# Sending the expert share with the routed row, and summing a token's four rows on TensorE

## The reference

```python
probs = softmax(x @ router_w + router_b)          # 16 experts
topw, topi = top_k(probs, 4)
topw = topw / sum(topw)
for each expert e:                                 # all of them on all tokens, in the reference
    acc += (gelu(x @ w1[e] + b1[e]) @ w2[e] + b2[e]) * combine[:, e]
x = layernorm(x + acc)
```

## Time and profile before

| | |
|---|---|
| median of 3 runs | 784.97 us (783.91 to 785.06) |
| the profiled execution | the page gives its span alone, 781.0 us from the first to the last instruction |
| PE / PEld busy | 583.7 us (75%) / 468.7 us (60%) |
| DVE busy | 576.7 us (74%) |
| ACT / POOL busy | 404.8 us (52%) / 348.8 us (45%) |
| DMA | 54.64 MB, 70 GB/s on the mean |

### The profile page before, as it was taken

How to read it: one execution, slowest core, us unless ns; L and a number is a source line. 1 busy time by engine, 2 the same in 40 slices (tenths; PEclk the granted TensorE clock), 3 DMA queues, 4 the chain that set the end, 5 groups by cost and what they waited for, 6 DMA issues and landing times.

```text
span 781.0 us, 18314 instructions
## 1 busy us (share of the span) xinstructions
PE 583.7 (75%) x4172; PEld 468.7 (60%) x4172; DVE 576.7 (74%) x1999; ACT 404.8 (52%) x1107; POOL 348.8 (45%) x445
## 2 busy tenths in 40 slices
PE   4576888778657899999999988239999999993000
PEld 1355666666546677777777756128888888883000
DVE  4888898898535788888988975676666666652998
ACT  1456654556224666666666653027666666663111
POOL 2611111011001137667667775637777777775000
PEclk9687787667656999999999985559999999998555
DMA  5000001000073012122121111243333333333653
GB/s 176 0 15 14 15 13 31 4 0 0 1 215 88 15 35 62 57 60 60 55 60 53 41 49 51 73 99 81 96 97 101 98 101 97 93 100 82 219 193 99
DMA packets 62705, 54.64 MB, mean 70 GB/s; under 512 B 16748, under 2 KB 52146, under 8 KB 62416
## 3 DMA queue, kind: packets, MB, share of 16 engines
q1 hardware_dynamic: 52816, 36.86, 17.1%
q0 software_dynamic: 8704, 16.87, 6.9%
q10 hardware_dynamic: 1152, 0.53, 0.3%
HBM read 29.96 MB, written 21.11 MB: 65 GB/s over the span
## 4 chain that ended last, share of the span: by engine, by line
PE 48%; DVE 19%; DMA 11%; issue 11%; SPq 4%; ACT 3%; POOL 2%; DVEq 1%; POOLq 0%; ACTq 0%
PE bank L781 6%; DMA ys<-yout,xin 5%; PE bank L788 4%; DMA xin<-xs 4%; PE bank L655 4%; PE bank L664 4%; PE bank L629 3%; PE bank L620 3%; DVE r L1450 3%; PE bank L646 3%; PE bank L539 3%; PE bank L773 2%; DVE Rq L1101 2%; DVE mx L1251 2%; PE bank L556 2%
## 5 line engine op out<-in xcount | busy, mean ns | idle before, releaser
L498 POOL DMA_INDIRECT ys<-yout,xin x144 | 145.8, 1013 | 54.4 <-issue 38.2
L479 POOL DMA_INDIRECT xs<-xrow,slots x128 | 130.5, 1019 | 50.7 <-issue 43.5
L996 ACT ACTIVATE hid<-bank,wcur 128x128 f32<-128x128 f32 x292 | 91.4, 364 | 41.1 <-PE bank L781 40.3
L781 PE MATMUL bank<-xinT,wcur 128*128 128x128 f32 x584 | 100.3, 295 | 0.6 <-issue 0.2
L1406 DVE COPY wcur<-wall 128x642 f32 x148 | 74.9, 508 | 20.9 <-DVE gates L1397 0.9
L788 PE MATMUL bank<-wcur,hid 128*128 128x128 f32 x576 | 88.5, 277 | 0.0
L1251 DVE TENSOR_REDUCE mx<-bank 128x4 f16<-128x308 f32 x128 | 60.0, 469 | 33.5 <-PE bank L629 31.9
L781 PEld LDWEIGHTS bank<-xinT,wcur 128*128 128x128 f32 x584 | 77.8, 194 | 8.5 <-issue 3.2
L1413 DVE TENSOR_TENSOR yout<-bank,wcur 128x128 f32<-128x128 f32 x144 | 42.0, 291 | 53.3 <-PE bank L788 51.9
L931 ACT ACTIVATE Ex<-bank 77x512 f32<-77x512 f32 x128 | 75.2, 588 | 5.1 <-PE bank L646 4.4
L788 PEld LDWEIGHTS bank<-wcur,hid 128*128 128x128 f32 x576 | 76.7, 194 | 0.0
(11 more groups left out here) (212 smaller groups left out, 1355.2 us busy)
## 6 DMA issues: line engine op xcount, KB each, us to landing
xin<-xs SPq DMA_DIRECT2D x156, 64.5 KB, 1.8
yin<-ys SPq DMA_DIRECT2D x16, 512.0 KB, 3.7
ys<-yout,xin POOLq DMA_INDIRECT x144, 2.3
xTg<-xT_dram SPq DMA_DIRECT2D x8, 256.0 KB, 2.8
X<-x_dram SPq DMA_DIRECT2D x1, 2048.0 KB, 8.3
x1s<-X SPq DMA_DIRECT2D x32, 64.0 KB
wall<-w_dram SPq DMA_DIRECT2D x1, 2048.0 KB, 8.5
X<-xrow SPq DMA_DIRECT2D x32, 64.0 KB
```

Of the source, the lines that this page charges most:

```text
L479: pool.indirect_dma_start(words, bass.IndirectOffsetOnAxis(ap=slots[p][:, r:r + 1], axis=0), xrow[p][:, r, 0:RW], None).then_inc(s(f"scatt ...
L498: pool.indirect_dma_start(ys, bass.IndirectOffsetOnAxis(ap=xin[p][:, :].bitcast(U32)[:, E:RW], axis=0), yout[p][:, :], None, bounds_check= ...
L781: mm = pe.matmul(psH[p % 3][:, c * P:(c + 1) * P], wcur[p % QUAD][:, c * P:(c + 1) * P], xinT[p % 4][:, :], start=True, stop=True)
L996: act.activation(hid[p % 3][:, c, :], psH[p % 3][:, c * P:(c + 1) * P], ACT.Gelu, bias=wcur[p % QUAD][:, 2 * I + c:2 * I + c + 1]).then_in ...
```

## The change

The share is carried with the row. `RW` becomes E + 2 = 130: column E keeps the row number and column E + 1 holds exp(logit - greatest logit), not yet divided by the sum. VectorE's copy into `topl` becomes a subtraction of the greatest logit, and ScalarE writes the exponential into `xrow` in a new piece `shares`, once per block; GpSimd's scatter waits for that too. In stage 3 VectorE computes b2 times the share for a tile (`b2u`, new) and then evicts psum times share plus `b2u` in one scalar_tensor_tensor. The rows in `ys` are thereby weighted.

In stage 4 TensorE sums the four weighted rows of a token: four matmuls with the identity as weights, 256 columns (two blocks) each, accumulated in one PSUM bank of four. VectorE multiplies the sum by the reciprocal sum of shares and adds `X`, takes the statistics and computes -mean x deviation (`nm3`); ScalarE normalises with Identity, scale and bias. `yin` gets six buffers in place of four, `r3`, `mv3`, `rs3` four, and all engines' programs of this stage are written out 16 times rather than looped. SP's order is: load f + 6, store f. Two of the VectorE instructions ahead of stage 3 and a wait between VectorE and ScalarE go.

```diff
-        RW = E + 1
+        RW = E + 2
...
             for f in range(YB):
                 load_y(f)
             for f in range(NF):
                 if f + YB < NF:
                     load_y(f + YB)
                 store(f)
...
                 pool.wait_ge(s("slots_ready"), b + 1)
+                pool.wait_ge(s("share_ready"), b + 1)
...
+            def expert_sum(f):
+                pe.wait_ge(s(f"y_in{f % YB}"), 16 * (f // YB) + 16)
+                free(pe, "gathered", FB * (f - 3))
+                for j in range(TOP):
+                    mm = pe.matmul(banks[f % 4][:, 0:FB * E].rearrange("p (c e) -> p c e", c=FB), ident[:, :], yin[f % YB][:, :, j * E:(j + 1) * E],
+                                   start=(j == 0), stop=(j == TOP - 1))
+                mm.then_inc(s("sum_ps"), 1)
...
+            def shares(i, c):
+                b, p = 4 * i + c, c % 4
+                act.wait_ge(s("top_saved"), b + 1)
+                act.activation(xrow[p][:, :, E + 1:E + 2], topl[:, bass.ds(b, 1), :].rearrange("p b k -> p k b"), ACT.Exp).then_inc(s("share_ready"), 1)
...
+            def scales3(f):
+                act.wait_ge(s("mv3_ready"), f + 1)
+                free(act, "rs3_ready", f - 1)
+                act.activation(ln3[f % 2][:, :], mv3[f % 4][:, :, 1], ACT.Ln, bias=EPS).then_inc(s("ln3_ready"), 1)
                 act.wait_ge(s("ln3_ready"), f + 1)
+                act.activation(rs3[f % 4][:, :], ln3[f % 2][:, :], ACT.Exp, scale=-0.5).then_inc(s("rs3_ready"), 1)
+            def normal3(f):
+                act.wait_ge(s("nm3_ready"), f + 1)
+                if f >= 2:
+                    act.wait_ge(s(f"out{f % 2}"), 16 * (f // 2))
+                for c in range(FB):
+                    ins = act.activation(o3[f % 2][:, c, :], r3[f % 4][:, c, :], ACT.Identity, scale=rs3[f % 4][:, c:c + 1], bias=nm3[f % 4][:, c:c + 1])
+                ins.then_inc(s("x3_ready"), 1)
+            for f in range(NF + 1):
+                if f < NF:
+                    scales3(f)
+                if f >= 1:
+                    normal3(f - 1)
...
-                    dve.tensor_copy(topl[:, bass.ds(route_n, 1), :], rtop[:, 0:TOP].unsqueeze(1)).then_inc(s("top_saved"), 1)
+                    dve.tensor_scalar(topl[:, bass.ds(route_n, 1), :], rtop[:, 0:TOP].unsqueeze(1), rtop[:, 0:1], None, ALU.subtract).then_inc(s("top_saved"), 1)
...
-            def results_out(i, written, p):
+            def results_out(i, loaded, written, p):
+                dve.wait_ge(s("w_ready"), i + 1)
+                dve.wait_ge(s(f"x_row_in{p}"), loaded)
+                dve.tensor_scalar(b2u[p % 2][:, :], wcur[p % QUAD][:, 2 * I + NI:WROW], xin[p][:, E + 1:E + 2], None, ALU.mult).then_inc(s("b2_ready"), 1)
                 dve.wait_ge(s("result_ps"), i + 1)
                 if written is not None:
                     dve.wait_ge(s(f"y_out{p}"), written)
-                dve.wait_ge(s("w_ready"), i + 1)
-                dve.tensor_tensor(yout[p][:, :], psY3[p % 3][:, 0:E], wcur[p % QUAD][:, 2 * I + NI:WROW], ALU.add).then_inc(s("y_ready"), 1)
+                dve.wait_ge(s("b2_ready"), i + 1)
+                dve.scalar_tensor_tensor(yout[p][:, :], psY3[p % 3][:, 0:E], xin[p][:, E + 1:E + 2], b2u[p % 2][:, :], ALU.mult, ALU.add).then_inc(s("y_ready"), 1)
...
+            def gather(f):
+                dve.wait_ge(s("sum_ps"), f + 1)
+                free(dve, "x3_ready", f - 3)
                 for c in range(FB):
+                    b = FB * f + c
+                    dve.scalar_tensor_tensor(r3[f % 4][:, c, :], banks[f % 4][:, c * E:(c + 1) * E], grec[:, b:b + 1], X[:, b, :], ALU.mult, ALU.add).then_inc(s("gathered"), 1)
...
+            def shift3(f):
                 dve.wait_ge(s("rs3_ready"), f + 1)
+                dve.scalar_tensor_tensor(nm3[f % 4][:, :], mv3[f % 4][:, :, 0], -1.0, rs3[f % 4][:, :], ALU.mult, ALU.mult).then_inc(s("nm3_ready"), 1)
+            for f in range(NF + 2):
+                if f < NF:
+                    gather(f)
+                if 0 <= f - 1 < NF:
+                    spread(f - 1)
+                if f < NF:
+                    stats(f)
+                if 0 <= f - 2 < NF:
+                    shift3(f - 2)
```

More of the change, by code:

```diff
@@ L340, in _, with load_y, store @@
             y4 = ys.rearrange("(b p k) e -> p b (k e)", p=P, k=TOP)
-            def load_y(f, p):
-                if not (isinstance(f, int) and f < 4):
-                    sp.wait_ge(s("r3_ready"), f - 3)
-                    pause(sp)
-                sp.dma_start(yin[p][:, :, :], y4[:, bass.ds(FB * f, FB), :]).then_inc(s(f"y_in{p}"), 16)
-            def store(f, p):
-                sp.wait_ge(s("x3_ready"), FB * f + FB)
-                pause(sp)
-                sp.dma_start(out[:, bass.ds(FB * f, FB), :], o3[p][:, :, :]).then_inc(s(f"out{p}"), 16)
-            for f in range(4):
-                load_y(f, f)
-            with sp.Fori(0, NF // 4 - 1) as i:
-                for p in range(4):
-                    load_y(4 * i + 4 + p, p)
-                    store(4 * i + p, p % 2)
-            for f in range(NF - 4, NF):
-                store(f, f % 2)
+            def load_y(f):
+                if f >= YB:
+                    sp.wait_ge(s("sum_ps"), f - YB + 1)
+                sp.dma_start(yin[f % YB][:, :, :], y4[:, FB * f:FB * f + FB, :]).then_inc(s(f"y_in{f % YB}"), 16)
+            def store(f):
+                sp.wait_ge(s("x3_ready"), f + 1)
+                sp.dma_start(out[:, FB * f:FB * f + FB, :], o3[f % 2][:, :, :]).then_inc(s(f"out{f % 2}"), 16)
+            for f in range(YB):
+                load_y(f)
+            for f in range(NF):
+                if f + YB < NF:
+                    load_y(f + YB)
+                store(f)
             for p in range(2):
@@ L799, in _ @@
                     outputs(UNROLL * i + d, d)
+            def expert_sum(f):
[5 more added lines that the diff above has]
+                mm.then_inc(s("sum_ps"), 1)
+            pe.wait_ge(s("xinT_ready"), NT + LEAD_T)
+            pe.wait_ge(s("hid_ready"), NI * (NT + LEAD_H))
+            pe.wait_ge(s("y_ready"), NT + 3)
+            for f in range(NF):
+                expert_sum(f)
         @block.scalar
@@ L955, in step @@
                     front(i, c + 3)
+                if there(i, c - 5):
+                    shares(i, c - 5)
                 if there(i, c - 1):
@@ L1390, in _ @@
                 dve.sem_inc(s("tables"), 1)
-            dve.wait_ge(s("top_saved"), B)
-            dve.tensor_tensor(gates[:, :, :], topl[:, :, :], topl[:, :, 0:1].to_broadcast([P, B, TOP]), ALU.subtract).then_inc(s("gates0"), 1)
             dve.wait_ge(s("gates1"), 1)
@@ L1396, in _ @@
             then(dve.reciprocal(grec[:, :], gsum[:, :]))
-            then(dve.tensor_tensor(gates[:, :, :], gates[:, :, :], grec[:, :].unsqueeze(2).to_broadcast([P, B, TOP]), ALU.mult))
             psY3 = banks[5:8]
@@ L1419, in _, with tiles @@
                     expert_weights(d, d, col[d])
-                def tiles(i, written):
+                def tiles(i, loaded, written):
                     for d in range(UNROLL):
@@ L1434, in _ @@
             for p in range(4):
                 dve.wait_ge(s(f"x2_saved{p}"), 16 * (B // 4))
-            Xf = X[:, :, :].rearrange("p b e -> p (b e)")
-            gf = gates[:, :, :].rearrange("p b k -> p (b k)")
-            def gather(f, d, loaded):
-                dve.wait_ge(s(f"y_in{d % 4}"), loaded)
-                if not (isinstance(f, int) and f < 2):
-                    dve.wait_ge(s("x3_ready"), FB * (f - 1))
-                for j in range(TOP):
-                    for c in range(FB):
-                        r = r3[d % 2][:, c, :]
-                        if j:
-                            dve.wait_ge(s("r3_steps"), TOP * FB * f + (j - 1) * FB + c + 1)
-                        prev = r if j else Xf[:, bass.ds((FB * f + c) * E, E)]
-                        dve.scalar_tensor_tensor(r, yin[d % 4][:, c, j * E:(j + 1) * E], gf[:, bass.ds((FB * f + c) * TOP + j, 1)], prev,
-                                                 ALU.mult, ALU.add).then_inc(s("r3_steps"), 1)
```

81 lines of the change are left out of this document (25 added, 56 removed).

## The result

The changed kernel is **8.5% slower**: median 850.65 us (849.53 to 852.39, four runs) beside 784.5 us (783.91 to 785.06, four runs) of the kernel before, run beside it; the ratio is 1.0847, interval 1.0831 to 1.0862. The forecast was 770 us.

| kernel, as profiled | stage 3 starts | last stage starts | end | stage 3 lasts | last stage lasts |
|---|---|---|---|---|---|
| before | 520.8 | 719.3 | 781.0 | 198.5 | 61.7 |
| after | 584.1 | 804.5 | 848.4 | 220.4 | 43.9 |
| difference | +63.3 | | +67.4 | +21.9 | -17.8 |

A forecast was written before the change was run, and what follows sets the result against it. VectorE was taken to bound the last stage and GpSimd the end of the expert stage. Span 781.0 - 18 + 3.5 = 766.5; with the median 4.0 above the span 770.5, stated as 770, range 762 to 779.

The forecast's parts named there:

- The last stage: Stage 4: work moved off VectorE, TensorE sums at 1.93 us a step; 17.7 us saved, rounded to 18.
- the lower clock: Last stage: TensorE, coming from idling, runs at the lower clock for 6 us, 1.6 steps.
- the cover: Expert stage: GpSimd's pace of about 1.3 us a tile hides VectorE's added work, nearly all used; +3 at 1.34.
- from 1.31 us per tile on: Expert stage, a rival: VectorE's pace or GpSimd lockouts decide; 1.38 to 1.40 a tile, +10 to +12, 777; chance 0.16.
- 1.26 to 1.35: Expert stage: VectorE's tile after the change, 1.26 us at best, 1.35 with another semaphore instruction or two.
- The +10: Expert stage: upper bound of the added time, at 1.38 us a tile; the lower bound was 0.
- The collision with GpSimd: Expert stage: added VectorE work lengthens each scatter by 0.02 us, 3 us over 144, partly inside the +3.
- The long scatter of the earlier trace: Kernel before, at 508.08: a scatter beneath a 2.35 us VectorE tensor_tensor took 2.68 us instead of 0.98.
- the outT copy: Cross-attention stage: its 0.43 us wait for TensorE swallows ScalarE's added 0.17 to 0.20 us per block; 0, at worst 6.4.
- the share is written a whole step earlier: Cross-attention stage: GpSimd's new wait before the four scatters finds the share already written; cost 0.
- the four rivals: Expert stage hides all, 764 (0.18); expert stage slows, 777 (0.16); last stage DMA-paced, 778 (0.08); low TensorE clock, 796 (0.05).
- the slower case: Last stage, a rival: TensorE's clock stays at or returns to the lower level, 3.7 us a step, 796; chance 0.05.

The follow-up runs named there:

- last stage alone: Changed kernel without shares in the expert stage (129-word rows, old eviction, unweighted sum): 768.31 us, ratio 0.9847; in a slow group 900.03, ratio 0.9751.
- no bias product: Changed kernel with shares moved to the end of ScalarE's step and b2 left out of the expert stage: 766.06 us beside 783.65, ratio 0.9793.
- shares next step: Changed kernel with a block's shares computed one step later, same place on ScalarE: 791.63 us, ratio 1.0104; in slow groups 909.67, 915.51 and 915.07.
- late shares: Changed kernel with shares moved to the end of ScalarE's step: 787.82 us beside 783.65, ratio 1.0041; in a slow group 907.9 beside 923.14.

## Why the prediction was wrong

**The last stage: right.** -17.8 for -18. A step is 1.73 where 1.93 stood; the lower clock lasted half as long as I took it (3 us from 808.4 for 6); loads took 5.0 us to land for 3.7, and TensorE waited for them 11.1 us in five waits, 8.9 of it the first. These nearly cancel, so that it is luck in part how close the sum came: first data to end 40.0 for "near 40".

**The expert stage: mechanism right, size wrong.** I saw that the cover was nearly used up and that VectorE would set the pace "from 1.31 us per tile on". The term that failed is the 1.26 to 1.35 of VectorE's tile; it is 1.47. The plain tile was right, 1.31 between 1.26 and 1.35. Of the pieces, copy to product took 0.56 in the mean for 0.40, product to eviction 0.42 for 0.37; eviction to copy was right, 0.49. Most of the difference sits in copy to product: with the scatters gone it is still 0.49, and the least is 0.41, so about 0.08 comes from the three tiles in twelve with a loop turn or a register load, and 0.07 from GpSimd's presence. That it is the turn and the loads is read from their places in the code; no run writes this loop out. I had counted one plain tile and taken it for the mean, though the kernel before shows the turn too: from copy to eviction at least 1.14 us there, at least 0.4 to 0.8 in the others. GpSimd, which ends the stage, went from 1.32 a tile to 1.47 (590.9 to 802.2 over 144): 0.15, times 144 is 22 us. The +10 that I gave as the upper bound was 0.12 above the low end of my own count, not a price of the worst case.

**The collision with GpSimd: not in the scatters.** Their mean fell from 1.013 to 0.995; 0.02 longer was forecast. The copies of VectorE took it, 0.51 to 0.58. The long scatter of the earlier trace rows, which I took as a sign, lay beneath a one-partition tensor_tensor and said little of these copies.

**The cross-attention stage: the step that failed.** "the outT copy after them waits 0.43 us for TensorE, which swallows it: 0, at worst 32 x 0.2 = 6.4", and "the share is written a whole step earlier: 0". I priced the instruction and took its wait as satisfied, because block c - 5 looked old by its number. It isn't: the routing of a block is late in VectorE's step, and VectorE's step runs beside the next step of the others. The timeline of the kernel before shows it, `Ex` at 383.11 and `topl` at 386.18, and I did not set the two against each other. Nor did I ask what is queued behind the waiting instruction: four `Ex`, and TensorE behind them. None of the four rivals had this wait, and the slower case was put in the last stage. The wait made a step 2.0 us longer (63.3 over 32 steps): about 1.2 of it at full clock (TensorE, busy 84.8 of 89.9 us before, had little slack), and the rest in the steps in which the clock fell behind the gaps.

**The rest** held: the padding and the written-out last stage show no cost (last stage alone: 197.3 and 43.8), nor do the longer rows (no bias product: 196.3). The span lay 2.3 us under the median for the 4.0 that I used.

## What to carry to other kernels

Of an instruction that is added to a pipeline, look up in the timeline when its operand is written and when the queue reaches it, both against one clock; the block number in the code does not tell it. Where an added instruction brings an engine near the pace of a tile, count a whole turn of the loop and not one plain tile: here a plain tile of 1.31 us stood for a mean of 1.47, and 0.28 us of work cost 0.15 us a tile beyond a slack that looked sufficient. An engine with slack can have the instruction for next to nothing. And where TensorE is nearly always busy at full clock, price a new gap twice: once as the gap, once as the clock that may follow it (here 1.2 us a step, and 1.0 to 1.4 more in the stretches where the clock fell).

## What was not expected of the hardware

- The same program took 784 us in some groups of runs and 920 to 936 in others, and chip number 15 stands at both levels. In shares next step the last stage is alike (44.5 and 44.2 us), stages 2 and 3 are longer. Stage 3, counted as in the table of stages, takes 261 to 270 us at the 930 level in every kernel with scatters, and 215 in the one without, less than the 220 of the changed kernel at the 784 level; yet a scatter itself is as short (median 982 ns). In the late shares there 31 of 143 tiles take 2.6 to 3.9 us and the others are as usual; without scatters none takes over 2.2. So the slowness of stage 3 goes with the scatters; how they cause it, and what sets the level, is open.
- Four f32 matmuls of 256 columns with their weight loads take 1.73 us a step at 2.4 GHz, 0.43 each; half of a 512-column one had been 0.48.
- The DMA engines moved 401 GB/s over 3.6 us, more than the 353 of the earlier trace rows.
